# A period of 56 tiles in place of 80 for the row tiles that SyncE and ScalarE fetch row by row

## What is computed

```python
# layer 0: three rounds, then an attention-weighted sum
def _wgc_layer(h, W, rel_w, heads, rels, tails):
    msg = rel_w[rels][:, None] * h[tails]
    agg = segment_sum(msg, heads, N_ENT) + h
    return tanh(agg @ W)
# layer 1: graph attention with 8 heads, softmax over each node's edges
# layer 2: mean over the incoming edges of x_nei[src] + edge_attr @ w_edge_W.T
out = segment_sum(x_nei[src] + edge_attr @ w_edge_W.T, dst, n)
return relu(x @ w_self_W.T + w_self_b + out / deg)
# layer 3: one of two weight matrices by the edge's type
msg = where((edge_types == 0)[:, None], Xs @ W_data.T + b_data, Xs @ W_control.T + b_control)
return relu(segment_sum(msg, dst, n) + X @ W_self.T + b_self)
```

## Time and profile before

| | |
|---|---|
| time of the runs, median | 9691.46 us |
| profiled execution: time, span | 9691.46 us, 9689.7 us |
| TensorE matmul busy | 4774.3 us (49%) |
| VectorE busy | 5181.3 us (53%) |
| ScalarE busy | 1743.6 us (18%) |
| GpSimd busy | 5832.6 us (60%) |
| mean granted TensorE clock | 0.662 of full speed |
| HBM read and written | 498.99 MB, 88.30 MB |
| row tiles fetched in the page's list of DMA issues | 1280 row DMAs each by SyncE into RING and RC and by ScalarE into RING and RC in the sum passes, 1280 by ScalarE in the mean pass, 640 for each of these four in the typed pass |

### The profile page before, as it was taken

The page is one execution under the profiler, slowest core; times in us unless marked ns, Lnnn a source line. Parts: engine busy times, 40 slices in busy tenths (PEclk is TensorE's granted clock), DMA queues, the critical chain, the costliest instruction groups (busy, mean ns, idle before and its releaser), DMA issues. The chain is left out here.

```text
span 9689.7 us, 102665 instructions
## 1 busy us (share of the span) xinstructions
PE 4774.3 (49%) x18373; PEld 3681.0 (38%) x18373; DVE 5181.3 (53%) x18170; ACT 1743.6 (18%) x5242; POOL 5832.6 (60%) x6135
## 2 busy tenths in 40 slices
PE   2333349544444444445656656767545555433233
PEld 2233247433333233333333334555445555422222
DVE  5645459555454545556676666666744445433333
ACT  2222237200000000004554533333300000100000
POOL 5666679655555555655666646666366666455554
PEclk7666679776777777677776665555566777755555
DMA  3322235211112111111111222222223333111111
GB/s 83 72 70 69 67 92 144 71 43 42 42 43 50 42 43 43 44 37 54 47 47 47 46 61 69 72 70 70 57 85 88 91 90 90 60 42 41 40 40 49
DMA packets 510333, 593.96 MB, mean 61 GB/s; under 512 B 134332, under 2 KB 401942, under 8 KB 509670
## 3 DMA queue, kind: packets, MB, share of 16 engines
q0 software_dynamic: 182688, 381.32, 14.2%
q1 hardware_dynamic: 313740, 202.45, 7.5%
q10 hardware_dynamic: 13258, 3.60, 0.2%
HBM read 498.99 MB, written 88.30 MB: 61 GB/s over the span
## 5 line engine op out<-in xcount | busy, mean ns | idle before, releaser
L2181 POOL DMA_INDIRECT RING<-TAB,IDX x1572 | 1488.4, 947 | 1093.6 <-issue 434.9
L1602 PE MATMUL PS<-RB,RING 128*128 128x256 f32 x4796 | 1458.3, 466 | 1338.2 <-issue 1034.2
L1602 PEld LDWEIGHTS PS<-RB,RING 128*128 128x128 f32 x4796 | 1086.2, 235 | 1706.7 <-issue 1212.3
L950 DVE TENSOR_TENSOR RA<-RA,PS 128x256 f32 x1612 | 666.2, 413 | 1224.2 <-remote 714.0
L2181 POOL DMA_INDIRECT RING<-TABM,IDX x810 | 765.8, 945 | 645.8 <-issue 229.0
L2181 POOL DMA_INDIRECT RING<-TABN,IDX x820 | 775.1, 945 | 557.1 <-issue 219.3
L2163 POOL DMA_INDIRECT ROWD<-RB,IDX x830 | 826.4, 996 | 444.1 <-issue 256.8
L2194 POOL DMA_INDIRECT RING<-TABQ,IDX x806 | 760.3, 943 | 483.7 <-issue 227.7
L950 DVE TENSOR_TENSOR RB<-RB,PS 128x128 f32 x1660 | 467.6, 282 | 881.5 <-remote 549.9
L1602 PE MATMUL PS<-OH,RING 128*128 128x128 f32 x2186 | 567.9, 396 | 453.7 <-DVE OH L936 183.3
L933 DVE TENSOR_SCALAR RB<-IOTA,KEY,WE 128x256 f32<-128x256 f32 x1612 | 712.6, 443 | 100.1 <-ACT RA L1931 42.3
(11 more groups left out here) (435 smaller groups left out, 9990.5 us busy)
## 6 DMA issues: line engine op xcount, KB each, us to landing
RC<-in_edge_attr_dram SPq DMA_DIRECT2D x830, 64.0 KB
RING<-ROWD SPq DMA_DIRECT2D x201, 264.0 KB
RB<-KRD SPq DMA_DIRECT2D x52, 512.0 KB
RA<-KRD SPq DMA_DIRECT2D x52, 512.0 KB
RING<-TAB,IDX POOLq DMA_INDIRECT x1572
RING<-TAB SPq DMA_DIRECT2D x1280, 0.5 KB
RING<-TAB ACTq DMA_DIRECT2D x1280, 0.5 KB
RC<-TAB ACTq DMA_DIRECT2D x1280, 0.5 KB
```

The lines of the kernel that those rows point to most:

```text
L950: v.tensor_tensor(sl, sl, sums_of(k, weighted), ALU.add).then_inc(s_ad, 1)
L1602: m = t_.matmul(sums_of(t, wide), rows, ramp, start=True, stop=True)
L2181: p.indirect_dma_start(GD[:, t % SLOTS, :], None, table, bass.IndirectOffsetOnAxis(ap=idx[:, t:t + 1], axis=0)).then_inc(s_ring[t // 4 % 1 ...
```

## The change

Three edits. `FETCH_EVERY` goes from 80 to 56, so that SyncE's tiles are 53, 109, ..., 781 and ScalarE's 55, 111, ..., 783: fourteen for each engine in a pass. The memset of `PLACES` goes. `put_places` takes the first column and the number of columns from the lists of tiles in place of constants; with fourteen tiles for each engine they are 28, 14 and 28 columns, as they were.

```diff
-FETCH_EVERY = 80
+FETCH_EVERY = 56
@@
             v.memset(work2, 1.0).then_inc(prep.sem, prep.one())
-            v.memset(PLACES[:, 0:10 * NTB], 0).then_inc(prep.sem, prep.one())
@@
             def put_places(k):
 
-                a, n = {SUM0 + 1: (PL_SRC, 4 * NTB), MEAN: (PL_MEAN, 2 * NTB), TYPED: (PL_TYPED, 4 * NTB)}[k]
+                n = len(fetched_in(k))
+                a = place_row(k, fetched_in(k)[0])
```

## The result

The changed kernel takes 10327.64 us (median of four runs, 10319.5 to 10332.16), the kernel before 9692.76 us beside it: 1.0655 times as long, 95% interval 1.0639 to 1.0672, or +635 us. I had forecast 10485 us, +792, within 10250 to 10720. The profiled execution took 10360.12 us, 32 more than the median, with a span of 10358.3 us; of the 21 executions on record, 10306 to 10360 us, it is the longest.

The account below looks back on a forecast made before the run. SyncE's issuing of single rows was taken to bound the sum and typed passes. Added were 229 + 203 + 207 for these passes, 33 for tails and 120 for the mean pass: +792 on 9691.5 us, 10485 us, range 10250 to 10720.

Parts of the forecast that it names:

- The bound: Sum and typed passes: SyncE's issuing of single rows sets the pace, about 126.9 us from one fetched tile to the next.
- The signs that I had named: Profile after: fourteen end-to-end SyncE tiles a pass; wrong if pauses, still 125 us a tile, or mean pass ending before 8300.
- The middle tiles: Fetched tiles between a pass's first and last: 105.4, 102.7 and 107.4 us each in first sum, second sum and typed pass.
- First and last tiles: Ends of SyncE's fetching in a pass: first tile 142 us with the gap, last 88, or 98 in the typed pass.
- The mean pass: ScalarE becomes the bound at about 91 us a tile; the pass ends at 8365 against 8244.5, +120 us.
- The edits at nothing: Memset removal and the longer slices in the same three DMAs at the start: no cost.
- the tails: Sum and typed passes: 16 more tiles worked off after the last fetched one, together +33 us.
- Rows as fast as beside 52 gathers: Rival: middle fetched tiles take 95.8 us, +396 in all, 10090 us; chance 0.12.
- the likeliest case: Whole kernel: the forecast itself, 10485 us, own range 10330 to 10650; chance 0.74.
- No speed-up: Rival: rows don't get faster with fewer gathers, fetched tiles stay at 126.9 us, about 11460 us; chance 0.08.
- GpSimd is the bound: Rival: fetches don't bound; removing 28 gathers saves 36 us, 9655 us; chance 0.04.
- The rule of the Trainium skill: Row DMAs on several engines: only issue time is saved, so at most the 36 us of the removed gathers is won.

Follow-up runs that it names:

- e10: Changed kernel with 64 row DMAs of 1024 bytes per fetched tile in place of 128 of 512, slow kind: 9318.36 us, ratio 0.9607 to the kernel before.
- e8: Kernel before with no row fetches, GpSimd gathering all tiles, slow kind: 9353.73 us against 9692.53, ratio 0.9643.
- e9: Kernel before with FETCH_EVERY at 120 in place of 80, slow kind: 9359.73 us, ratio 0.9648.
- e6: Changed kernel itself run again against the kernel before, slow kind: 10253.07 us against 9635.5, ratio 1.0653.
- e11: Kernel before with the period of 56 in the mean pass alone, slow kind: 9685.96 us against 9627.85, ratio 1.0057.
- e1: Changed kernel with the memset of PLACES put back, quick kind: 8021.12 us against 8053.72 for the kernel before, ratio 0.9955.
- e2: Kernel before with no row fetches, GpSimd gathering all tiles, quick kind: 8131.46 us, ratio 1.0095.

## Why the prediction was right, and where its sizes were off

**The bound.** Right, for the chips of the slow kind, of which the trace was one. SyncE's row issue bounds the sum and typed passes: halving its DMAs (e10) takes 935 us or more away, and more gathers on GpSimd (e8, e9) make the kernel faster. The signs that I had named came too, the last of them narrowly: the mean pass's last attribute load ends at 8723 us, and as the pass begins 408 us later than before, that is 8315 by the clock of the prediction, which had put the sign of being wrong under 8300. That the time itself lies in the range is due in part to a choice that I didn't make: the first comparison ran on the slow kind as well.

**The middle tiles.** Right in kind, too dear in size. Start to start they took 100.9 us in the first pass (from 1944.24 to 3155.41, twelve tiles), where I had 105.4, 101.0 in the second, where I had 102.7, and 104.8 in the typed pass, where I had 107.4. The passes grew by 176, 185 and 172 us for 229, 203 and 207. The mis-sized term is the number of rows left when the last of the 54 gathers is issued, 56 of 128 in the first pass. In the kernel after 82 rows are out at that point, so 46 are left (a timeline of SyncE, and a window of line 2180):

```profile
2144.47 79.59 SPq L406 DMA_DIRECT2D RC<-TAB  x82
```

```profile
2144.00:2224.60 80.60, 50.22 (x54) 0.75 0.16 44
```

Ten rows at 0.4 us and the 2 us that I added for gathers in flight are 6 us, of which 4.5 show. The quick rate starts with the last gather, so the 2 us were not needed. The 72 rows issued came from one tile, and it was a low one: cut in the same way, the eight middle tiles of that pass in the kernel before give 70 to 81, those of the second pass 73 to 84, and the twelve of the first pass of the kernel after 75 to 83. Why the number differs from tile to tile is open. In the typed pass the build itself, 103.3 us a tile, meets the 103.4 measured, and the 2.7 us that I put on top for its long later tiles are the miss. A straight line through the tiles with 78 and 109 gathers (125.6 and 160.1 us) would have given 98.9 for 54.

**First and last tiles.** 139.7 us with the gap for 142, and 91.2 for 88; 96.5 for 98 in the typed pass.

**The mean pass.** It became a bound, as said: thirteen waits, 164 us, and ScalarE without a pause. From the third on its tiles took 85 to 91 us for my 89.4, for instance

```profile
7719.16 85.09 ACTq L406 DMA_DIRECT2D RC<-TABN  x128
```

and the pass grew by 71 us, not 120: 35 of the 49 lie in the tiles, the rest in the end, where the last attribute load comes 36 us after the last fetched row, and I had 50. On two other chips the growth, against the same 1320 us, was 44 us (e6, e11), so this term was nearly three times too large there.

**The edits at nothing.** The memset is one instruction of VectorE at 1.7 us that takes 0.12 us:

```profile
L506 DVE MEMSET AD<- x1: 117/117/117, 1.7 to 1.7; 128x70 int32 x1
```

The spans differ by 669 us, the four passes by 604. Of the other 64 us, 8 lie ahead of the first pass, 14 between the sum passes, 25 between the second and the mean pass and 17 behind the typed pass, where I had 33 for the tails. The 31 us over are about what this execution took over the median, 32; that they are the same is likely, and not shown.

**The rivals.** "Rows as fast as beside 52 gathers" was nearly as near as my own in a middle tile, 5.1 us under the 100.9 of the first pass where I was 4.5 over, and farther off in the time: 10090 is 238 us under the 10328 measured, 10485 is 157 over. The measured time lies just under the likeliest case's own range, which began at 10330. "No speed-up" fell. "GpSimd is the bound" fell here and is the truth on the quick kind: there a fetched tile takes 51 us, under the 67.5 us that I had named as the point from which it decides, and e1 is 33 us faster than the kernel before for the 36 that I had worked out. The rule of the Trainium skill (DMA: Bandwidth & Descriptors, Rules for kernel authors), that DMAs from several engines bring no bandwidth and only save issue time, fits there: 33 us (23 to 49) were gained, and the issue time of the 28 gathers removed is 35.

**What the prediction couldn't see.** One trace shows one chip. My chance of 0.04 for faster was a chance about the mechanism; that the mechanism itself could change with the chip was in none of the cases.

## What to carry to other kernels

When an engine issues many small DMAs one by one to relieve another, time a whole batch beside the work it relieves. The batch must fit in the time between two points where it is waited for, with its rate beside that work and not its rate alone. A balance found between two issuing engines can have its sign turned by the chip it runs on, so measure it on more than one before it is set.

## What was not expected of the hardware

Between chips, the same kernel differs by a fifth (8054 to 9693 us). The row fetches are the smaller part of it: without them it is still 8131 against 9354 us (e2, e8). On the quick kind 128 row DMAs take 51 us beside gathers at full pace, 2.5 rows a us; on the slow kind SyncE's tiles of 128 take 76 to 182 us, the more gathers beside them the longer, and they come to the quick kind's rate when GpSimd stands (48 rows in 19 us). The gathers themselves are busy for 0.948 us on both. Waits that the trace puts down to "remote" stand on the slow kind ahead of VectorE and ScalarE too (VectorE's additions of line 950 in the kernel before: 714 us in 116 waits), and on the quick kind, in e1 and e2, there is none on any engine; so it isn't a matter of GpSimd and SyncE alone. What slows SyncE's instructions and makes GpSimd's 233 pauses on the slow kind is open: "remote" names no source, and no experiment separated the chip from what else it may have been doing.
